# Toeplitz attention stage: 12 block products for 16 in the lower left square, and the second norm's statistics from a running sum and a Square pass

## What is computed

```
x = x + tanh(g_xattn) * gated_conv(ctx, ctx, layernorm(x), ssm_kernel, D)
x = x + tanh(g_ffn) * moe(layernorm(x))            # 8 experts, top 2, with LoRA

# gated_conv, with heads of 8 rows and L = 1024:
kv  = k_i[l] * v_j[l]                              # k = v = ctx
y   = causal convolution of kv with the head's kernel (fft of 2L) + D * kv
out_j[l] = sum_i y_ij[l] * q_i[l]
```

## Time and profile before

| | |
|---|---|
| median of 3 runs | 1708.61 us |
| profiled execution | 1702.75 us |
| its span | 1700.9 us |
| PE matmuls busy | 1553.1 us, 91% |
| DVE busy | 1232.6 us, 72% |
| ACT busy | 538.7 us, 32% |
| POOL busy | 948.3 us, 56% |
| convolution matmuls (line 584) | 6912 |
| mean DMA rate | 206 GB/s |

### The profile page before, as it was taken

One profiled execution on the slowest core, in us unless ns is written; L12 is line 12 of the kernel. 1 busy time (PEld: TensorE's weight loads), 2 busy tenths in 40 slices (PEclk: granted clock), 3 DMA queues, 4 the chain that ended last, 5 costly groups with the idle time before them and its releaser, 6 DMA issues. The chain is left out here.

```text
span 1700.9 us, 32688 instructions
## 1 busy us (share of the span) xinstructions
PE 1553.1 (91%) x11300; PEld 1494.9 (88%) x11301; DVE 1232.6 (72%) x1829; ACT 538.7 (32%) x848; POOL 948.3 (56%) x633
## 2 busy tenths in 40 slices
PE   5999999999999999999999999747999999996553
PEld 5999999999999999999999999647999999895332
DVE  4878888888888888888888888594444444444798
ACT  3333433333343334333333433203333333331000
POOL 6667757766775776577567757052222222232465
PEclk9999999999999999999999999857999999998586
DMA  5554554555455555545554554234788888885999
GB/s 182 166 178 158 172 170 163 177 177 175 154 170 167 173 165 189 165 152 174 173 176 157 181 167 146 79 133 137 251 291 311 288 305 292 299 276 196 411 396 360
DMA packets 101006, 350.84 MB, mean 206 GB/s; under 512 B 11953, under 2 KB 12465, under 8 KB 100977
## 3 DMA queue, kind: packets, MB, share of 16 engines
q1 hardware_dynamic: 71024, 241.39, 42.5%
q0 software_dynamic: 29952, 109.07, 18.0%
HBM read 236.58 MB, written 113.84 MB: 206 GB/s over the span
## 5 line engine op out<-in xcount | busy, mean ns | idle before, releaser
L584 PE MATMUL Y<-kvhi,t_hi 128*128 128x288 f32 x2304 | 689.4, 299 | 3.2 <-DMA t_lo<-klo 1.9
L584 PE MATMUL Y<-kvlo,t_hi 128*128 128x288 f32 x2304 | 679.9, 295 | 0.0
L584 PE MATMUL Y<-kvhi,t_lo 128*128 128x288 f32 x2304 | 679.8, 295 | 0.0
L584 PEld LDWEIGHTS Y<-kvhi,t_hi 128*128 128x128 f32 x2304 | 433.0, 188 | 4.9 <-DMA t_lo<-klo 2.3
L584 PEld LDWEIGHTS Y<-kvlo,t_hi 128*128 128x128 f32 x2304 | 433.7, 188 | 0.0
L584 PEld LDWEIGHTS Y<-kvhi,t_lo 128*128 128x128 f32 x2304 | 433.5, 188 | 0.0
L440 DVE TENSOR_REDUCE oT<-z 128x128 f32<-128x1280 f32 x256 | 379.5, 1482 | 6.7
L269 POOL TENSOR_TENSOR kvlo<-kv,kvhi 128x1152 fp32r<-128x1152 f32 x128 | 341.3, 2691 | 4.1 <-ACT kvhi L306 4.1
L423 DVE TENSOR_TENSOR z<-Y,qT 128x512 f32<-128x512 f32 x256 | 175.9, 687 | 174.1 <-PE Y L584 174.1
L258 POOL TENSOR_TENSOR kv<-cT 128x1024 f32<-128x1024 f32 x128 | 291.7, 2279 | 8.7 <-DMA cT<-in_c 8.7
L306 ACT CAST kvhi<-kv 128x1152 fp32r<-128x1152 f32 x128 | 148.5, 1161 | 303.3 <-POOL kv L261 303.3
(11 more groups left out here) (151 smaller groups left out, 2149.8 us busy)
## 6 DMA issues: line engine op xcount, KB each, us to landing
made_rows<-made POOLq DMA_DIRECT2D x72, 512.0 KB
t_hi<-khi SPq DMA_DIRECT2D x64, 512.0 KB, 3.9
t_lo<-klo SPq DMA_DIRECT2D x64, 512.0 KB, 5.1
cT<-in_c SPq DMA_DIRECT2D x32, 768.0 KB, 6.4
x_nat<-in_x SPq DMA_DIRECT2D x32, 512.0 KB, 4.1
x<-x_new SPq DMA_DIRECT2D x32, 512.0 KB, 4.9
normed<-n SPq DMA_DIRECT2D x32, 512.0 KB, 3.0
w_raw<-in_w SPq DMA_DIRECT2D x32, 384.0 KB, 4.1
```

What stands on the lines that cost most here:

```text
L584: mm = nc.tensor.matmul(Y[s2][:, a, 0:YC], t[h][:, w], m[h][:, s, :], start=(s == 0 and t is t_hi and m is kvhi), stop=(s == c and t is t_lo))
```

## The change

Write the lower left square of a head's Toeplitz matrix (output blocks 4 to 7, input blocks 0 to 3) as 2 by 2 squares of 2 by 2 blocks. With A the square on its diagonal, B the one below it and C the one above, the outputs are A x0 + C x1 and B x0 + A x1. The changed kernel computes A (x0 - x1) once (`shared`, 4 block products, into OP), and (C + A) x1 and (B + A) x0 (`summed`, 4 block products each, accumulated in Y with the pair's other products). The first pair is then Y + shared, the second Y - shared; DVE joins them in place in PSUM before the multiply. So 12 block products stand for 16, and a half-tile has 32 block products for 36.

What follows from it in the code:
- **Start**: the sum of the kernel row and itself 2 blocks on (ksum, 768 columns) is made, split, and written to `kshi` and `kslo`. krow and its parts now lie in z and kvhi[1], kvlo[1]. The zeroing of z comes after them.
- **SP**: `windows` loads four pieces, t_hi and t_lo of 768 columns and u_hi and u_lo of 640.
- **POOL and ACT**: kv is one buffer for both h. The square terms (the group with shift 0) are made by ACT (`squares`, Square of cT), POOL's wide multiply has three groups left. POOL adds `difference` (kv blocks 0, 1 less 2, 3; 128x576) and `low_difference`; ACT adds `high_difference`. ACT copies the shared product from OP to `common[h]` (`take_common`), in each tile before `high_w` and again before the next tile's head.
- **DVE**: four joins a tile in `multiply` (n = 1 and 2), each with a wait on `joined` before the multiply.
- **Order**: ORDER is (1, 2, 3, 0), so the pairs have 7, 7, 11 and 3 block products. `transpose_o(i-1)` stands behind conv(i,0,0), `transpose_n2(i-1)` behind conv(i,1,0), `transpose_x(i+1)` before conv(i,1,3). Shared stands before conv(i,h,0). On DVE, residual, low_n2 and the statistics of the next tile are moved accordingly.
- **Second norm**: bn_stats and bn_aggr of x_new are gone. `residual` gives the row's sum (accum_out); ACT makes the sum of squares of x_new less its mean by a Square pass with accum_out, into n2 as scratch, then the root.

```diff
-ORDER = (1, 2, 0, 3)
+ORDER = (1, 2, 3, 0)
@@ SP
+                eng.dma_start(kshi_d, ksum_hi.bitcast(F32)).then_inc(k_out, 16)
+                eng.dma_start(kslo_d, ksum_lo.bitcast(F32)).then_inc(k_out, 16)
-                eng.wait_ge(k_out, 32)
+                eng.wait_ge(k_out, 64)
...
+                    eng.dma_start(t_hi[h][:].bitcast(F32), kernel_window(khi_d, n, KW, TW)).then_inc(t_in[h], 16)
+                    eng.dma_start(t_lo[h][:].bitcast(F32), kernel_window(klo_d, n, KW, TW)).then_inc(t_in[h], 16)
+                    eng.dma_start(u_hi[h][:].bitcast(F32), kernel_window(kshi_d, n, KS, SW)).then_inc(t_in[h], 16)
+                    eng.dma_start(u_lo[h][:].bitcast(F32), kernel_window(kslo_d, n, KS, SW)).then_inc(t_in[h], 16)
@@ POOL
+                def difference(n):
+                    eng.wait_ge(square_done, 2 * n + 1)
+                    if not (isinstance(n, int) and n < 1):
+                        eng.wait_ge(diffhi_done, n)
+                    nc.gpsimd.tensor_tensor(diff[:], kv[:, 0:2, :], kv[:, 2:4, :], ALU.subtract).then_inc(diff_done, 1)
+                def low_difference(n, h):
+                    eng.wait_ge(diffhi_done, n + 1)
+                    nc.gpsimd.tensor_tensor(diff_lo[h][:], diff[:], diff_hi[h][:].bitcast(F32),
+                                            ALU.subtract).then_inc(difflo_done[h], 1)
                 def head(i, p, h, have):
-                    products(2 * i + h, h, 0, p, have)
-                    products(2 * i + h, h, 1, p, have)
+                    products(i, h, 0, p, have)
+                    products(i, h, 1, p, have)
+                    difference(2 * i + h)
...
                     low_kv(2 * i + h, h)
+                    low_difference(2 * i + h, h)
@@ ACT
+                def squares(n, p, h):
+                    eng.wait_ge(kv_done, 2 * n + 1)
                     for half in range(2):
...
+                        nc.scalar.activation(kv[:, c0:c0 + NC // 2, 0:IB], cT[p][:, h, c0:c0 + NC // 2, 0:IB],
+                                             ACT.Square).then_inc(square_done, 1)
+                def head(n, p, h):
+                    squares(n, p, h)
+                    high_kv(n, h, 0)
+                    high_kv(n, h, 1)
+                    high_difference(n, h)
+                def take_common(n, h):
+                    eng.wait_ge(shared_ready, n + 1)
...
+                    nc.scalar.copy(common[h][:], shared_y).then_inc(common_done, 1)
+                def root2(i, p):
+                    eng.wait_ge(res_done, i + 1)
+                    nc.scalar.mul(low2[:], sum2[:], -1.0 / L).then_inc(n2sd_done, 1)
...
+                    nc.scalar.activation(n2[p][:], x_new[p][:], ACT.Square, bias=low2[:, 0:1],
+                                         accum_out=square2[:]).then_inc(n2sd_done, 1)
+                    eng.wait_ge(n2sd_done, 4 * i + 2)
+                    nc.scalar.activation(sd2[:], square2[:], ACT.Sqrt, bias=epsc[:, 0:1], scale=1.0 / L).then_inc(n2sd_done, 1)
                 def body(i, p, first=False, last=False):
+                    take_common(2 * i, 0)
                     high_w(i)
-                    high_kv(2 * i + 1, 1)
+                    head(2 * i + 1, p, 1)
+                    if not first:
+                        root2(i - 1, 1 - p)
+                        normalize2(i - 1, 1 - p)
                     if not (isinstance(i, int) and i < 2):
                         take_small(i - 2)
...
+                    take_common(2 * i + 1, 1)
                     if not last:
+                        head(2 * i + 2, 1 - p, 0)
                         root(i + 1)
...
@@ DVE
+                    if n in (1, 2):
+                        eng.wait_ge(common_done, 2 * i + h + 1)
+                        nc.vector.tensor_tensor(y, y, common[h][:], (ALU.add, ALU.subtract)[n - 1]).then_inc(joined, 1)
+                        eng.wait_ge(joined, 4 * i + 2 * h + n)
@@ PE
+                def shared(i, h):
+                    eng.wait_ge(t_in[h], 64 * i + 64)
+                    eng.wait_ge(difflo_done[h], i + 1)
...
+                    for a in range(2):
+                        for c in range(2):
+                            mm = block(OP[:, a * HALF:a * HALF + YC], t_hi[h], t_lo[h], 4 + a - c, diff_hi[h], diff_lo[h], c,
+                                       start=c == 0, stop=c == 1)
+                    mm.then_inc(shared_ready, 1)
...
+                        if n == 1:
+                            summed(out, h, 2 + a, 2, start=True)
+                            summed(out, h, 1 + a, 3, start=False)
+                        if n == 2:
+                            summed(out, h, 4 + a, 0, start=True)
+                            summed(out, h, 3 + a, 1, start=False)
+                        for s in range(0 if n in (0, 3) else NC // 2, c + 1):
+                            mm = plain(out, h, c - s, s, start=s == 0)
...
+                    shared(i, 0)
+                    conv(i, 0, 0)
+                    if not first:
+                        transpose_o(i - 1, 1 - p)
+                    conv(i, 0, 1)
+                    conv(i, 0, 2)
+                    if not (isinstance(i, int) and i < 2):
+                        project(i - 2)
+                    conv(i, 0, 3)
+                    shared(i, 1)
+                    conv(i, 1, 0)
+                    if not first:
+                        transpose_n2(i - 1, 1 - p)
+                    conv(i, 1, 1)
+                    conv(i, 1, 2)
                     if not last:
                         transpose_x(i + 1)
+                    conv(i, 1, 3)
```

More of the change, by code:

```diff
@@ L143, in attend @@
         kvlo_done = [sem(f"kvlo_done{h}") for h in range(HT)]
+        square_done = sem("square_done")
+        diff_done, diffhi_done = sem("diff_done"), sem("diffhi_done")
+        difflo_done = [sem(f"difflo_done{h}") for h in range(HT)]
+        shared_ready, common_done = sem("shared_ready"), sem("common_done")
+        joined = sem("joined")
         y_ready = sem("y_ready")
@@ L531, in body @@
                         eng.wait_ge(st_done, 3 * i + 4)
-                    total(i, p, 0, 3)
+                    multiply(i, p, 1, 0)
                     if not last:
                         aggregate(i + 1)
-                    if not (isinstance(i, int) and i < 2):
-                        take_lr(i - 2)
-                    multiply(i, p, 1, 0)
+                    total(i, p, 1, 0)
+                    if not first:
+                        low_n2(i - 1)
+                    multiply(i, p, 1, 1)
                     if not last:
                         invert(i + 1)
-                    total(i, p, 1, 0)
-                    multiply(i, p, 1, 1)
                     total(i, p, 1, 1)
                     multiply(i, p, 1, 2)
-                    if not first:
-                        low_n2(i - 1)
                     total(i, p, 1, 2)
@@ L579, in conv @@
                     for a in range(2):
-                        c = 2 * r + a
-                        for s in range(c + 1):
-                            w = slice((c - s) * P, (c - s + 1) * P)
-                            for t, m in ((t_hi, kvhi), (t_hi, kvlo), (t_lo, kvhi)):
-                                mm = nc.tensor.matmul(Y[s2][:, a, 0:YC], t[h][:, w], m[h][:, s, :],
-                                                      start=(s == 0 and t is t_hi and m is kvhi),
-                                                      stop=(s == c and t is t_lo))
+                        out = Y[n % 2][:, a, 0:YC]
+                        c = 2 * ORDER[n] + a
+                        if n == 1:
[6 more added lines that the diff above has]
+                            mm = plain(out, h, c - s, s, start=s == 0)
                     mm.then_inc(y_ready, 1)
```

209 lines of the change are left out of this document (113 added, 96 removed).

## The result

| | before | after |
|---|---|---|
| median | 1708.61 us (1705.83 to 1708.88, 4 runs) | 1725.97 us (1722.34 to 1730.03, 4 runs) |
| profiled execution, span | 1702.75, 1700.9 us | 1722.34, 1720.4 us |
| mean granted clock over the span | 0.95 | 0.929 |
| convolution matmuls | 6912 | 6144 |

The changed kernel is slower: 1.0106 times the time before, 95% interval 1.0074 to 1.0138. I had forecast 1694.4 us. The time is just inside my range (1664 to 1726), but on the side to which I gave a chance of 0.20.

What follows compares the result with a forecast made beforehand. PE's stream bound the kernel; after the change, POOL's chain would hold the tile at 32.5 us against 33.27. Gain 17.7 us, start included, less 3.5 at the end, is 14.2: 1708.6 to 1694.4 us, range 1664 to 1726.

Steps and rivals of the forecast that it cites:

- the clock in PE's new gap: Rival: the clock falls behind PE's wait before the second half's shared products, 1.7 us a tile, 1747 us; chance 0.07.
- The wait for xn: PE's wait before the transposes of xn near the tile's end: 0.35 us a tile.
- The mechanism that I expected to eat the gain: POOL's kv chain, started only after the first half's shared products, makes PE wait 2.0 us before shared(i,1) in every tile.
- first shared product: Start of the kernel: PE's first convolution work needs diff_lo, low_difference ending at 25.9; before, the first conv started at 21.29.
- tile 1 starts: Start of the second tile: at about 58.5 us against 53.5 before, 5.0 lost.
- PE idle at the end: End of the convolutions: DVE's last reduction ends 2.4 us later after PE than before, when it was 3.2 after.
- low_kv's rate: POOL's difference, 128x576: 1.44 us at this rate, against the 1.37 taken.
- DVE's later last reduction: End of the convolutions: join, multiply and reduction of the 11-block pair make it end 2.4 us later after PE.
- the Square at the end: End of the convolutions: the Square behind take_small costs about 1.1 us, part of the 3.5 lost there.
- the chain doesn't bind: Rival: POOL's chain is short enough that the tile falls to PE's own 30.1 to 30.5 us, about 1632; chance 0.10.
- The dear POOL steps: Rival: POOL's 128x576 steps cost 2.1 us each, chain 18.8, tile 33.9, 1738 us; chance 0.09.
- A reload for Square: Rival: ACT's Square and Sqrt need different tables, the load delays xn by 1.3 us a tile, 1735 us; chance 0.03.

Runs made afterwards that it cites:

- fill_gap: The changed kernel with 16 needless matmuls per tile, from the second tile on, before PE's wait for diff_lo of the second half: 1699.99 us, ratio 0.9957 to before.
- norm_only: The kernel before with the second norm's part alone (residual with accum_out, Square pass on ACT, no bn_stats of x_new): 1707.71 us, 0.9999.
- fill_half: The changed kernel with 8 needless matmuls per tile before PE's wait for diff_lo of the second half: 1699.66 us, 0.9958 to before.
- w_first: The changed kernel with ACT's high_w one place earlier, before take_common, nothing else: 1653.92 us, 0.9682 to before.
- w_last: The changed kernel with POOL's low_w behind the head of h = 1 instead of before it, nothing else: 1654.85 us, 0.9683 to before.
- blocks_only: The changed kernel with the second norm's part undone (bn_stats and bn_aggr of x_new back on DVE, no Square pass): 1745.68 us, 1.0219 to before.
- fill_quarter: The changed kernel with 4 needless matmuls per tile before PE's wait for diff_lo of the second half: 1702.04 us, 0.9969 to before.
- w_last_bn: The changed kernel with POOL's low_w behind the head of h = 1 and the second norm's part undone: 1733.57 us, 1.0158 to before.

## Why the prediction was wrong

**Step that failed: the clock in PE's new gap.** I named it as a rival, gave it 0.07, and left it out of the sum. I put its limit "anywhere from a gap of 1.4 to 3", my gap at 2.0, and then reasoned as if 2.0 were on the safe side. Nothing in the rows said so: they had 1.38 without a fall and 3.2 with one, and 2.0 lies between. By these rows, with the limit anywhere between, the chance was about one in three. What the runs showed: at this place 2.0 to 2.2 us of idle time cost the clock in 18 of the 30 ordinary tiles, 1.7 us or less in none. That is 24 us, and it turned a gain of about 6 us into a loss (fill_gap has 1699.99 against 1706.64, the kernel after 1725.97 against 1708.61).

**Its price.** I said 1.7 us a tile, from half of 3.4. It measured 1.31: in 3.35 us at 0.24 us a load instead of 0.13 PE loses 1.5, and 0.2 is given back, as PE comes later to the next wait (a gap of 2.17 instead of 2.37). The wait for xn, 0.3 us in the tiles without a fall, is gone in those with one, but 0.35 ahead of the next transposes of o stands in its place. By my 1.7 in all tiles it would have been 1747; with 18 of 30 tiles at 1.31 it is 24 us, and 1725.97 less 24 is 1702.

**What was right.** The mechanism that I expected to eat the gain did, in most steps to a tenth of a microsecond:

| step | predicted | measured |
|---|---|---|
| take_common ends, from the tile's start | 2.35 | 2.4 |
| w_lo starts | 3.2 | 3.2 |
| PE starts shared(i,1) | 17.6 | 17.65 |
| gap, idle | 2.0 | 2.0 to 2.2 |
| tile with the clock kept | 32.5 | 32.6 |
| PE's wait for xn | 0.35 | 0.3 and less, in 11 tiles |
| DVE a tile | 29.1 of 32.5 | 29.1 of 33.4 (261.58 of 300 us) |
| wide multiply of POOL | 1.76 | 1.856 |
| difference | 1.37 | 1.446 |
| low_difference | 1.44 | 1.433 |
| join | 0.75 | 0.762 |
| first shared product | 25.9 | 25.23 |
| tile 1 starts | 58.5 | 59.99 |
| PE idle at the end | 3.2 + 2.4 | 5.59 |

The durations of the unknown operations, from the groups of the kernel after (busy us, mean ns, idle time before):

```profile
L498 DVE TENSOR_TENSOR Y<-Y,common 128x576 f32<-128x576 f32 x128 | 97.5, 762 | 26.3 <-PE Y L640 26.3
L285 POOL TENSOR_TENSOR kv<-cT 128x768 f32<-128x768 f32 x128 | 237.5, 1856 | 8.7 <-DMA cT<-in_c 8.7
L296 POOL TENSOR_TENSOR diff<-kv 128x576 f32<-128x576 f32 x64 | 92.5, 1446 | 3.7 <-ACT kv L346 3.7
L423 ACT ACTIVATE n<-x_new,low 128x1024 f32<-128x1024 f32 x31 | 35.8, 1153 | 1.2
```

**Smaller misses.** The difference goes at low_kv's rate, which I had as the other bound. The two wide multiplies are 0.1 each dearer than by my rate; a half's products took 2.25 us (633.32 to 635.57) instead of 2.14. With them POOL's chain ends at 17.58 instead of 17.4; PE starts 0.07 behind it, where I had allowed 0.2, and that evens it out. Tile 1 starts 1.5 us late, because the gap in tile 0 is 5.07 start to start and leaves the clock low behind it, which I had charged only for PE's first 3.3 us.

**The sum, set against the profiled execution.** I had the last convolution end at 1064.8; it ends at 1095.1. Of the 30.3 us, 24 are fallen clocks, 1.5 the start, 2.2 tile 1 (34.8 instead of 32.6), and 3 that the other tiles take 32.6 instead of 32.5; these rounded terms make 30.7. From there to the end of the span it is 625.3 us, against 618.4 before. 2.4 us of this are DVE's later last reduction, as predicted, and 1.1 I had put down to the Square at the end. The other 3.4 I can't place; norm_only, which has nothing of the block products, has 623.5 there, and the stretch differs by as much between kernels that are alike in it (625.0 in fill_gap, 628.3 in fill_half). That stays open. Against this, the median after lies 3.6 us above its profiled execution, where I had taken 5.9.

**The rivals.** That the chain doesn't bind fell (the gap is there), though w_first and w_last show what it was worth: 1654, and not 1632, because xn is late next, and 1611 only with three more places mended. The dear POOL steps fell by the rows just shown. A reload for Square fell: ACT loads no table between its Square passes and roots, and norm_only is at 0.9999. The page "ScalarE: Activation LUTs" of the Trainium skill, section "Table sets: the hidden batching unit", has a load only where the set changes; by that rule, the trace puts Square and Sqrt in one set. What I left out altogether is how much of the new order hung on the norm part; I costed it as 1.4 us less on DVE in covered time, and it holds the order together (blocks_only).

**What stays open.** Why the same gap costs the clock in one tile and not in the next isn't settled. In the kernel after neither its length nor the tile's number decides it, and the two executions differ in which tiles fall; in blocks_only 2.3 us always cost it and 2.0 seldom; in fill_half 2.81 us once didn't; and 2.0 us ahead of the transposes of xn are nearly always harmless. Whether the place, the work around the gap or its moment in time makes the difference wasn't tried.

## What to carry to other kernels

A new wait on the engine that sets the time is priced twice: by its length, and by what the clock does behind it. If the gap lies between the longest that the trace shows as harmless and the shortest that it shows as costly, its price belongs in the forecast, with a share by where it lies between the two (here about one third; 18 of 30 tiles paid it). When a change shortens the bounding engine's work, first follow the chain that feeds it and take everything off its head that only stands there by habit (here one cast and one subtraction for weights that nobody awaited); a single swap of two lines turned 1% slower into 3% faster. A part that measures as neutral on the old kernel can carry the new one, so it is tested on both.

## What the runs showed of the hardware that I had not expected

- A granted clock that falls behind the gaps ahead of the shared products in 20 and 22 of 32 tiles of two executions (2.0 to 2.2 us idle, more in the first two tiles), stays behind 1.7 us and less in all 30 ordinary tiles of fill_half and of fill_quarter, and stays behind 2.0 us ahead of the transposes of xn in 40 of 41 (w_last_bn and blocks_only). When it falls, the pace is 0.24 us a load instead of 0.13 for some 3.35 us.
- In 17 of the 18 ordinary tiles of the first execution the fall comes after the restart, by up to 1.6 us: PE's first load behind the gap (612.04) still had 0.19 us, the second 0.29 and the third 0.33. In one tile the first load has 0.29, so there the clock fell as the gap ended:

```profile
346.06 0.29 PEld L638 LDWEIGHTS OP<-diff_hi,t_hi 128*128 128x128 f32 x1 [2.19 <-issue]
```

- Matmuls without use are a remedy: 4 of them (0.57 us) ahead of the wait bring back 22 us (1724.27 to 1702.04).
- A join in place in PSUM, 128x576, costs 0.762 us, 1.32 ns a column, and a multiply with one operand in PSUM 1.35 (0.69 for 512): so no extra cost of writing back to PSUM shows. Square with accum_out over 128x1024 costs 1.153 us and 0.185 for reading the accumulator; the residual's sum costs 0.083.
